# A new opening for a fused attention and mixture-of-experts kernel: the first tiles in another order and in other banks

## The reference, cut to what matters

```
x = x + layernorm(attention(layernorm(x)))     # x: 8 batches x 256 rows x 256
x = x + layernorm(ffn(layernorm(x)))           # 8 experts, 2 per row, and a shared one

def attention(x):                              # 16 heads of q, 4 of k and v, D = 128
    q, k, v = split(x @ w_qkv.T)
    q = layernorm(q, qn_g, qn_b); k = layernorm(k, kn_g, kn_b)   # over each head's 128
    q = q * cos + rotate_half(q) * sin         # the same for k
    w = softmax(causal(q @ k.T / sqrt(D)))     # 4 heads of q share a head of k and v
    return (w @ v) @ w_o.T
```

## Time and profile before

| | us |
|---|---|
| median of 3 runs | 673.3 |
| lowest, highest | 671.51, 673.95 |
| the profiled execution | 668.37 |
| its span, first to last instruction | 666.4 |
| TensorE busy in it | 629.9 (95%) |
| VectorE, ScalarE, POOL busy | 553.0, 553.6, 530.0 |

### The profile page before, as it was taken

One profiled execution on the slowest core, in us unless ns is written; L12 is line 12 of the kernel. 1 busy time (PEld: TensorE's weight loads), 2 busy tenths in 40 slices (PEclk: granted clock), 3 DMA queues, 4 the chain that ended last, 5 costly groups with the idle time before them and its releaser, 6 DMA issues.

```text
span 666.4 us, 15665 instructions
## 1 busy us (share of the span) xinstructions
PE 629.9 (95%) x4518; PEld 586.2 (88%) x4518; DVE 553.0 (83%) x1918; ACT 553.6 (83%) x2111; POOL 530.0 (80%) x601
## 2 busy tenths in 40 slices
PE   6879999999999999999999999999799999999993
PEld 5658898999999999999999999999689889999981
DVE  4889999898899889899898999979999745555476
ACT  3589999999999999999999999999898536666643
POOL 3798898999899899989989998999877425666554
PEclk9999999999999999999999999999999999999997
DMA  8001306997650000000000000000437033444273
GB/s 333 30 0 34 104 1 196 334 335 220 4 47 0 2 1 0 2 1 1 2 1 1 1 1 2 1 1 26 144 122 228 33 100 104 128 129 121 78 254 126
DMA packets 51122, 54.27 MB, mean 81 GB/s; under 512 B 19840, under 2 KB 42752, under 8 KB 50912
## 3 DMA queue, kind: packets, MB, share of 16 engines
q1 hardware_dynamic: 47632, 43.90, 23.9%
q0 software_dynamic: 3408, 9.38, 3.8%
HBM read 23.83 MB, written 29.51 MB: 80 GB/s over the span
## 4 chain that ended last, share of the span: by engine, by line
PE 67%; POOL 12%; DVE 10%; ACT 5%; issue 4%; DMA 1%; SPq 0%; POOLq 0%; ACTq 0%; DVEq 0%
PE pQ L460 7%; PE pQ L461 7%; PE pQ L462 7%; PE pPO L460 4%; PE pPO L566 4%; PE pPO L461 4%; PE pPO L462 4%; PE pT L538 4%; PE pSS L460 3%; PE pA L460 3%; PE pA L461 2%; PE pA L462 2%; PE pSS L461 2%; POOL ropes L1993 2%; PE pSS L462 2%
## 5 line engine op out<-in xcount | busy, mean ns | idle before, releaser
L1002 ACT ACTIVATE P<-P,nmx 128x128 f32<-128x128 f32 (+1 forms) x256 | 118.8, 491 | 1.0 <-DVE nmx L1451 1.0
L460 PE MATMUL pQ<-W 128*128 128x512 f32 (+2 forms) x334 | 116.2, 348 | 2.1 <-DVE W L1365 0.8
L461 PE MATMUL pQ<-W 128*128 128x512 f32 (+2 forms) x334 | 111.6, 334 | 0.0
L462 PE MATMUL pQ<-W 128*128 128x512 f32 (+2 forms) x334 | 111.3, 333 | 0.0
L1993 POOL TENSOR_TENSOR ropes<-ropes 128x640 f32<-128x640 f32 x63 | 99.3, 1576 | 13.8 <-DVE ropes L1428 13.4
L1010 ACT ACTIVATE P<-P,rinv 128x128 f32<-128x128 f32 (+1 forms) x256 | 105.7, 481 | 2.1 <-DVE rinv L1457 2.1
L2003 POOL TENSOR_TENSOR ropes<-ropes 128x640 f32<-128x640 f32 x63 | 99.5, 1579 | 4.9
L460 PE MATMUL pPO<-W 128*128 128x256 f32 (+1 forms) x323 | 94.9, 294 | 5.6 <-DVE W L1466 3.6
L987 ACT ACTIVATE ropes<-pQ 128x128 f32<-128x128 f32 x320 | 88.5, 303 | 9.7 <-PE pQ L462 9.7
L461 PE MATMUL pPO<-W 128*128 128x256 f32 (+1 forms) x323 | 91.4, 283 | 0.0
L462 PE MATMUL pPO<-W 128*128 128x256 f32 (+1 forms) x323 | 91.2, 282 | 0.0
(11 more groups left out here) (276 smaller groups left out, 2174.5 us busy)
## 6 DMA issues: line engine op xcount, KB each, us to landing
xs<-stage SPq DMA_DIRECT2D x1, 17550.0 KB, 58.4
stage<-xs SPq DMA_DIRECT2D x39, 130.0 KB, 2.4
ropes<-in_ew SPq DMA_DIRECT2D x8, 608.0 KB, 4.9
stage<-in_wqkv SPq DMA_DIRECT2D x3, 768.0 KB, 8.9
stage<-ys SPq DMA_DIRECT2D x4, 512.0 KB, 6.5
ropes<-ys SPq DMA_DIRECT2D x4, 512.0 KB, 7.0
out<-X SPq DMA_DIRECT2D x7, 256.0 KB, 2.0
X<-in_wo SPq DMA_DIRECT2D x1, 1536.0 KB, 12.6
```

The source lines that it names most:

```text
L460: e.matmul(out, lh, rh, start=start, stop=False, skip_group_check=True)
L461: e.matmul(out, lh, rl, start=False, stop=False, skip_group_check=True)
L462: return e.matmul(out, ll, rh, start=False, stop=stop, skip_group_check=True)
L1002: a = e.activation(P[:, z, span(t)], P[:, z, span(t)], ACT.Exp, bias=nmx[:, z, t:t + 1], scale=-1.0, accum_out=sums[:, z, t:t + 1])
```

## The change

The steps 0 to 7 are no longer a loop but a list written out for each engine, and the loop starts at OPEN = 8.

- **Transfers**: constants first, then the first half of group 0, x of batch 0, the second half, gains, cos and sin.
- **Zeros**: VectorE clears a block `still`, and TensorE multiplies it with itself eight times into pT before anything else.
- **Tile 1** has its qkv in the score banks pSS (`pQu`), right behind tile 0's in pQ. VectorE's end of tile 1 is cut into `rope_add` and `rope_scale`, and it counts in `s_rope_d` (`wait_rope`). POOL makes tile 1's root before its own multiplication for tile 0.
- **Transposes**: rounds 0 to 3 are those of (1,0), (1,1), (0,0), (0,1), in that order (`ROUND`, `rnd`), and rounds 1 and 3 go to bank pA instead of pT (`pTr`).
- **Centring**: i = 2 to 4 within the list, after qkv of the tiles 0 and 1; 5, 6 and 7 in the steps 8, 9 and 10, all in pPO (`pW`); each waits for the wq_lo that frees its bank (`WFREE`). Group 2's second half and group 3 are therefore centred after the first score.
- **The rest**: qkv(3, 0) and (3, 1) stand behind scores(0) in step 8; bias_table1 moves ahead of tile 0's rotation; the gains' scaling on ScalarE moves behind wq_hi(1); the statistics of batch 1 move from step 6 to step 9.

```
-CENTRE = {0: [2], 1: [3], 3: [4, 5], 5: [6], 6: [7]}
-HI = {1: [2], 2: [3], 4: [4], 5: [5], 6: [6], 7: [7]}
-LO = {2: [2], 3: [3], 4: [4], 5: [5], 6: [6], 7: [7]}
+OPEN = 8
+CENTRE = {8: [5], 9: [6], 10: [7]}
+SPLIT = {8: [5], 9: [6], 10: [7]}
+WFREE = {2: 2, 4: 3, 5: 5, 6: 6, 7: 7}
+ROUND = {(1, 0): 0, (1, 1): 1, (0, 0): 2, (0, 1): 3}
...
+
+def stats_step(s):
+
+    return 0 if s == 9 else s // 16 if s > 16 and s % 16 == 6 and s // 16 + 1 < NB else None
+
+
+def rnd(u, r):
...
+        pW = [(pPO if i in (1, 2, 4, 5, 6, 7) else pSS)[:, 0:GW] for i in range(2 * HKV)]
+        pQu = [pSS if u == 1 else pQ for u in range(NU)]
+        pTr = [pA if i in (1, 3) else pT for i in range(2 * NU)]
...
-            e.dma_start(X[:, 0:2, :], x_d[:, 0:2, :]).then_inc(s_dx[0], 16)
             e.dma_start(const[:, 0:256], const_d[:, 0:256]).then_inc(s_dconst, 16)
             e.dma_start(raw_q[0][:, 0, :], wqkv_d[:, 0, 0, :]).then_inc(s_dwq[0], 16)
+            e.dma_start(X[:, 0:2, :], x_d[:, 0:2, :]).then_inc(s_dx[0], 16)
+            e.dma_start(raw_q[0][:, 1, :], wqkv_d[:, 0, 1, :]).then_inc(s_dwq[1], 16)
             e.dma_start(gb[:, :, :], gb_d).then_inc(s_dgb, 16)
-            e.dma_start(raw_q[0][:, 1, :], wqkv_d[:, 0, 1, :]).then_inc(s_dwq[1], 16)
             e.dma_start(cs[:, :, :, :], cs_d).then_inc(s_dcs, 16)
             for g in range(1, HKV):
                 e.dma_start(raw_q[g], wqkv_d[:, g, :, :]).then_inc(s_dwq[g + 1], 16)
...
-                if i >= 2:
-                    e.wait_ge(s_wqlo, i - 1)
+                if i == 3:
+                    e.wait_ge(s_v, 2)
+                elif i >= 2:
+                    e.wait_ge(s_wqlo, WFREE[i])
...
-                if u > 0 and y == 0:
+                if u == 1:
+                    e.wait_ge(s_wqlo, 1)
+                elif u == 2:
+                    e.wait_ge(s_v, 1)
+                elif u > 2 and y == 0:
                     e.wait_ge(s_t2, 2 * u - 1)
-                if u > 0 and y == 1:
+                elif u > 2:
                     e.wait_ge(s_v, u)
                 if u == UPLACE and y == 1:
                     places(0)
...
             def qk_T(u, r):
                 h0, n = ROUNDS[r]
+                i = rnd(u, r)
                 if r == 0:
-                    e.wait_ge(s_rope, u + 1)
-                if 2 * u + r > 0:
-                    e.wait_ge(s_qT, 2 * u + r)
+                    wait_rope(e, u)
+                if 2 <= i < 4:
+                    e.wait_ge(s_qT, i - 1)
+                elif i >= 4:
+                    e.wait_ge(s_qT, i)
+                out = pTr[i]
                 for i in range(n):
                     h = (h0 + i - 1) % 5
-                    p = e.transpose(pT[:, i * 128:i * 128 + 128], t1[:, u % 3, h * D:h * D + D], ident)
+                    p = e.transpose(out[:, i * 128:i * 128 + 128], t1[:, u % 3, h * D:h * D + D], ident)
...
-                    e.wait_ge(s_wqlo, 2 * HKV - 1)
+                    e.wait_ge(s_wqlo, 4)
...
+            def keep_running(n):
+
+                for i in range(n):
+                    e.matmul(pT[:, 0:128], still, still, start=True, stop=True, skip_group_check=True)
+
+            e.wait_ge(s_still, 1)
+            keep_running(8)
             centre(0)
+            centre(1)
             ln1_T(0)
-            centre(1)
-            for s in range(WOVEN):
+            qkv(0, 0)
+            qkv(0, 1)
+            qkv(1, 0)
+            qkv(1, 1)
+            centre(2)
+            centre(3)
+            qk_T(1, 0)
+            qk_T(1, 1)
+            qk_T(0, 0)
+            centre(4)
+            qk_T(0, 1)
+            qkv(2, 0)
+            qkv(2, 1)
+            for s in range(OPEN, WOVEN):
                 n = s - LS
                 tu, tr = divmod(s - 5, 2)
-                if s < QFIRST:
-                    qkv(s // 2, s % 2)
-                if 0 <= tu < NU:
+                if 2 <= tu < NU:
                     qk_T(tu, tr)
+                if is_head(s, 0):
+                    scores(n)
+                if s == OPEN:
+                    qkv(3, 0)
+                    qkv(3, 1)
                 for i in CENTRE.get(s, []):
                     centre(i)
-                if is_head(s, 0):
-                    scores(n)
-                if QFIRST <= s < 2 * NU:
+                if s < 2 * NU:
                     qkv(s // 2, s % 2)
                 if is_head(s, 6):
                     out_proj(n - 6)
...
-                if u >= 2 and y == 0:
-                    e.wait_ge(s_rope, u - 1)
+                if u == 3 and y == 0:
+                    e.wait_ge(s_rope_d, 1)
...
+            wq_hi(0)
+            wq_hi(1)
             e.wait_ge(s_dgb, 16)
             e.activation(gb[:, 0:2, :], gb[:, 0:2, :], ACT.Copy, scale=float(D) ** -0.5).then_inc(s_gain, 1)
-            wq_hi(0)
             ln1_hi(0)
-            wq_hi(1)
-            for s in range(WOVEN):
+            rope(0, 0)
+            rope(0, 1)
+            rope(1, 0)
+            rope(1, 1)
+            wq_hi(2)
+            spread(0)
+            spread(1)
+            wq_hi(3)
+            qT_hi(1, 0)
+            qT_hi(1, 1)
+            qT_hi(0, 0)
+            qT_hi(0, 1)
+            wq_hi(4)
+            rope(2, 0)
+            rope(2, 1)
+            rope(3, 0)
+            for s in range(OPEN, WOVEN):
                 n = s - LS
                 tu, tr = divmod(s - 5, 2)
-                if QFIRST <= s <= 2 * NU:
+                if s <= 2 * NU:
...
-                    rope((s - 1) // 2, (s - 1) % 2)
-                if 0 <= tu < NU:
+                if 2 <= tu < NU:
                     qT_hi(tu, tr)
...
-                for i in HI.get(s, []):
+                for i in SPLIT.get(s, []):
                     wq_hi(i)
-                if s in (2, 3):
-                    spread(s - 2)
...
-            def rope_end(u):
+            def rope_add(u):
+
+                z, z3 = u % 2, u % 3
+                e.wait_ge(s_t2, 2 * u + 2)
+                e.tensor_tensor(t1[:, z3, :], t1[:, z3, :], t2[:, z, :], ALU.add).then_inc(s_rope_d, 1)
+
+            def rope_scale(u):
 
...
-                e.wait_ge(s_rope, u)
-                e.tensor_tensor(v3, v3, TB[:, u % 2, :, :], ALU.add).then_inc(s_rope, 1)
+                e.tensor_tensor(v3, v3, TB[:, u % 2, :, :], ALU.add).then_inc(s_rope_d, 1)
...
+            e.memset(still, 0.0).then_inc(s_still, 1)
             ln1_stats(0)
+            wq_lo(0)
             ln1_apply(0)
-            wq_lo(0)
+            wq_lo(1)
             ln1_lo(0)
-            wq_lo(1)
             scale_tables1()
-            for s in range(WOVEN):
+            bias_table1()
+            rope(0, 0)
+            rope(0, 1)
+            rope(1, 0)
+            rope(1, 1)
+            rope_add(1)
+            wq_lo(2)
+            rope_scale(1)
+            qT_lo(1, 0)
+            wq_lo(3)
+            qT_lo(1, 1)
+            qT_lo(0, 0)
+            qT_lo(0, 1)
+            wq_lo(4)
+            rope(2, 0)
+            rope(2, 1)
+            soft_max(0)
+            rope(3, 0)
+            for s in range(OPEN, WOVEN):
                 n = s - LS
                 tu, tr = divmod(s - 5, 2)
                 if is_head(s, 2):
                     ln2_lo(fb)
                 if 0 <= fb < NB - 2 and fs == 14:
                     logit(fb)
-                if 0 < s < QFIRST:
+                if 2 <= tu < NU:
+                    qT_lo(tu, tr)
+                if s <= 2 * NU:
                     rope((s - 1) // 2, (s - 1) % 2)
-                if 0 <= tu < NU:
-                    qT_lo(tu, tr)
-                if QFIRST <= s <= 2 * NU:
-                    rope((s - 1) // 2, (s - 1) % 2)
-                if is_head(s, 0):
+                if is_head(s, 0) and n > 0:
                     soft_max(n)
-                if s % 16 == 6 and s // 16 + 1 < NB:
-                    ln1_stats(s // 16 + 1)
+                if stats_step(s) is not None:
+                    ln1_stats(stats_step(s) + 1)
...
-                if s == 2:
-                    bias_table1()
-                if s == 4:
-                    rope_end(1)
-                for i in LO.get(s, []):
+                for i in SPLIT.get(s, []):
                     wq_lo(i)
...
+                if u == 0:
+                    root(5, ss[:, 1, :], rs[:, 1, :], 1.0 / D, (s_sq, 4), s_qvar, s_rs, 1)
                 e.wait_ge(s_add, k)
                 e.wait_ge(s_rs, u + 1)
                 e.tensor_tensor(v3, v3, rs[:, z, :].unsqueeze(2).to_broadcast([128, 5, D]),
                                 ALU.mult).then_inc(s_mul, 1)
-                if u == 0:
-                    root(5, ss[:, 1, :], rs[:, 1, :], 1.0 / D, (s_sq, 4), s_qvar, s_rs, 1)
...
-            for s in range(WOVEN):
-                if s == 2:
-                    rope(0)
-                if QFIRST <= s <= 2 * NU and (s - 1) % 2 == 1:
+            rope(0)
+            rope(2)
+            for s in range(OPEN, WOVEN):
```

(9 more changed lines are left out.)

43 lines of the change are left out of this document (23 added, 20 removed).

## The result

The changed kernel takes 681.4 us (median of its four runs; 672.4 before, also of four), where 676.7 were forecast and 680.3 was the upper end of the range. The comparison gives a ratio of 1.0112 with an interval of 1.0082 to 1.0141: slower by 7.5 us (5.5 to 9.5), where 3.4 were forecast. One execution of the changed kernel took 788.67 us, far from the others, and is left out of the comparison. The two medians differ by more than the ratio says, by 9.0 us, or 8.6 without that execution; with four runs of each the ratio and its interval are what counts. The profiled execution took 680.98 us, 12.6 more than that of before.

A forecast was written before the change was run, and what follows sets the result against it. VectorE, without slack from step 12, was taken as the bound of the opening; step 12 at 52.0 instead of 48.58 gave +3.4 us, so the median of 673.3 becomes 676.7 us, range 671.3 to 680.3.

The forecast's parts named there:

- The bound, and where to read the shift: VectorE without slack from step 12's reciprocal: each microsecond it comes later is one of the run; 52.0 against 48.58.
- Steps (1) to (3): Transfers, zeros and the way to the first qkv: centre(1) at 7.9, qkv(0,0) at 11.8, first rotation at 14.6 us.
- the prediction's own sign of going wrong: It goes wrong if the first qkv starts before 11 us, or if centre(7) is not the stall.
- Step (4): Two tiles at once: rope_scale(1) slowed by POOL, as 2.08 against 0.81 us; tile 1 ready at 23.8 us (25.9 before).
- Step (5): Transposes: qk_T(1,0) at 23.85, qkv(2,0) 27.2 to 28.7, scores(0) at 29.4, 5.3 us earlier than before.
- The rival of the slow array: Clock falls to 1.2 GHz in TensorE's gaps before qkv(0,0): +2.9 us on the chain, 679.6; chance 0.14.
- Step (6): Work put off: qkv(3,0) at 31.4, VectorE idle 2.6 us before step 9, centre(7) at 44.1, step 12 at 52.0.
- The zeros: Eight matmuls at TensorE's start, hidden under the wait for data: cost nothing; centre(0)'s ten passes in 1.3 us.
- The head start survives: Rival: VectorE's idle times swallow the work put off, scores(0)'s lead of 5.3 us reaches step 12: 668.0; chance 0.10.
- From the profile to the median: Profiled execution lies 4.9 us below the median of the runs: 671.8 for the changed kernel becomes 676.7.

The follow-up runs named there:

- e2_rows: c2_spread with POOL's scaling of batch 1's rows in step 8, directly behind their root, instead of step 11: ratio 1.0029 to the kernel before.
- a1_fill: The changed kernel with 29 more matmuls of zeros in TensorE's waits of the opening: ratio 1.0059 to the kernel before.
- a4_cold: The changed kernel without the eight matmuls of zeros at its start: ratio 1.0112 to the kernel before.
- a2_order: The changed kernel with centre(7) behind qkv(5,0) on TensorE instead of ahead of it: ratio 1.0065 to the kernel before.
- c2_spread: c1_group2 with centre(6), its splits and batch 1's statistics in step 8, and centre(7) in step 9: ratio 1.0015 to the kernel before.
- e3_tile2: e2_rows with tile 2 ahead of tile 0's transposes, the other engines' lists to match: ratio 1.0006 to the kernel before.
- b1_zeros: The kernel before with only the eight matmuls of zeros, and their clearing, added at its start: ratio 0.9986.
- c1_group2: The changed kernel with zeros in TensorE's waits, centre(7) behind qkv(5,0), and centre(5), wq_hi(5), wq_lo(5) ahead of tile 3: ratio 1.0026 to before.
- The repeat: The changed kernel again, unedited, in another session on another chip: ratio 1.0100 to the kernel before.

## Why the prediction was right or wrong

**The bound, and where to read the shift: right for the changed kernel.** The loss is made before VectorE's step 12 and is carried unchanged (6.17 at head 6, 6.12 at head 114); at step 12 it was 5.83. As a rule for any opening it failed: e2_rows opened step 12 0.4 sooner than before and ran 1.5 late, since POOL had become the bound behind it.

**Steps (1) to (3): right at their end, in part by luck.** The first half of the weights and x came as worked out (centre(0) began at 4.58, right behind the zeros, for 4.7; the statistics of x at 5.47 for 5.7). The second half came 1.3 us sooner: centre(1) at 6.56 for 7.9, and with it qkv(0,0) at 10.86 for 11.8. That is the prediction's own sign of going wrong, a first qkv before 11 us. The clock then fell in qkv(0,0), and the two errors, one each way, left the first rotation 0.4 late.

**Step (4): right within 0.1.** POOL's last add and `rope_scale` contend as foreseen: 2.04 for the operation beside POOL's 1.99, tile 1 ready at 23.88 (23.8). The Trainium skill, GPSIMD Engine Reference, section 1 Specifications, has the two contend for SBUF when VectorE's instruction has two inputs there; this second pair of rows agrees.

**Step (5): wrong, and this is where the missing 2.9 us are.** The sum has centre(4) and qkv(2,0) at the full clock: it put the clock's fall behind TensorE's wait at nothing. Tile 1's first transposition waits from 20.88 to 23.93 for `rope_scale`, 3.05 us, a wait that follows from the prediction's own numbers (centre(3) over at 20.7, tile 1 ready at 23.8) but that it doesn't name. Behind it the clock is at the half to about 31.3 us: centre(4) takes 2.34 for 1.28, and qkv(3,0) starts at 34.29 for 31.4. a1_fill shows the cause: products of zeros in TensorE's waits of the opening, nothing else changed, bring centre(4) to 1.28, qkv(3,0) to 31.36 and centre(7) to 44.02. Which of the waits it takes isn't separated; in a4_cold the clock fell before the long one.

**The rival of the slow array: its mechanism right, its price right by luck, its place and its chance wrong.** It was to cost 2.9 us in the gaps before qkv(0,0), in centre(1), the transposes of x and qkv(0,0), with a chance of 0.14, as a case beside the forecast. Centre(1) took 1.38, at the full clock. The clock did fall in qkv(0,0), from the first pass at 10.86, and its result was read at 13.82 (13.5); VectorE waited 0.66 us there, and in a1_fill, without this fall, tile 1's first transposition came only 0.3 us sooner (23.64). The costly fall came at the wait named above, in centre(4) and qkv(2,0), which the rival didn't price; that it cost 2.9 as well is chance. And it excluded nothing: a fall of the clock adds to the forecast's sum, 3.4 + 2.9 = 6.3, against 6.2 in the trace. The error was to give a term of the sum as an alternative to the sum. The evidence used against it, a wait of 1.28 after which the clock stood, said nothing of one more than twice as long, nor of several in a row.

**Step (6): right.** The order of the stalls, the 2.6 us of VectorE and the stall ahead of the last centre are there, each shifted by some 2.9, and 2.4 at step 12. Moving qkv(5,0) out from behind the last centre (a2_order) won 0.9, so its place in the queue was only that part of the loss.

**The zeros:** centre(0)'s ten passes went from 2.50 to 1.38, as forecast. That was not sure: of the ten traces with these zeros, five have 1.38 or 1.40 and five 1.89 to 2.22 (a1_fill, a2_order, c2_spread, e2_rows, e3_tile2). On before alone they are worth 0.9 us at most (b1_zeros).

**"The head start survives": wrong, for the reason given.** The first score came 2.4 us sooner than before, and the work put off ate that and more. With the clock held up, c1_group2 to e3_tile2 took the work put off back step by step and brought the offset from 2.5 to 1.5, 1.3, 1.5 and 0.8 us: level with before, no more. The last two steps, 1.5 and 0.8, are of the third session, where the changed kernel's own offset was 0.5 higher. The limit went from centre(7)'s place to POOL, which makes three passes over every tile and can't start tile 2 sooner than TensorE and VectorE deliver it.

**From the profile to the median: wrong.** I took the changed kernel's profiled execution to lie as far below its median as before's, 4.9 us. It lay 0.4 below. The changed kernel's has the loss of some 6 us after 470 us, which goes with the session; before's has not, and was the fastest of its kernel (668.37, the others 670.63 to 673.95). Of the measured 7.5 us, 6.2 are shown to come from the opening; the other 1.3 lie within the interval, and no cause of them is shown. The repeat agrees: 6.7 us by its ratio, 6.7 by its opening.

## What to carry to other kernels

Walk the planned timeline once more for the gaps alone: wherever the engine of matrix products waits for some three microseconds, or has several shorter waits in a row, price what follows at the half clock, and put it into the sum, not beside it. A piece of work brought forward gains only what the engines without slack are spared; here the first score came earlier and the work put off for it came due on VectorE and POOL at their tightest. A wait filled with products of zeros holds the clock up, but the fill is worth trying only where the work behind the wait is long and on the path. And before a late stretch that nobody edited is explained, look whether other kernels of the same session show the same loss there.
